# Fourteen tiles of the last feed-forward: rounding the hidden rows one slot later, behind a maximum

## What is computed

```
x = x + cross_attention(layernorm(x), ctx)      # 16 heads of 16, keys and values from the 1601 context rows
x = x + gated_recurrence_and_ff(layernorm(x))   # conv, linear recurrence, gated feed-forward
x = x + bitlinear(gelu(bitlinear(layernorm(x), w1)), w2)

def bitlinear(x, w):                            # the inner rows are 1024 wide
    scale = 127 / max(|x|, per row)
    return (round(x * scale) clipped / scale) @ ternary(w).T
```

## Time and profile before

| | |
|---|---|
| median of 3 runs | 2118.18 us (2115.8 to 2119.51) |
| the profiled execution | 2124.54 us, its span 2122.7 us |
| granted TensorE clock, mean | 0.986 of full speed |
| PE busy | 1970.8 us (93%) |
| DVE busy | 1287.4 us (61%) |
| ACT busy | 1050.8 us (50%) |
| POOL busy | 672.6 us (32%) |

### The profile page before, as it was taken

One profiled execution on the slowest core, in us unless ns is written; L12 is line 12 of the kernel. 1 busy time (PEld: TensorE's weight loads), 2 busy tenths in 40 slices (PEclk: granted clock), 3 DMA queues, 4 the chain that ended last, 5 costly groups with the idle time before them and its releaser, 6 DMA issues.

```text
span 2122.7 us, 72750 instructions
## 1 busy us (share of the span) xinstructions
PE 1970.8 (93%) x31780; PEld 1587.3 (75%) x31796; DVE 1287.4 (61%) x2276; ACT 1050.8 (50%) x1532; POOL 672.6 (32%) x1349
## 2 busy tenths in 40 slices
PE   6799999999999999999999999999999998999987
PEld 4577777777778787787878778787777777777764
DVE  3555656756656665766656575665656666565644
ACT  3444455555465555455555544555544444444441
POOL 4323333423233332333324233342323232122301
PEclk8999999999999999999999999999999999999999
DMA  5533434343333343434333425242342321213122
GB/s 185 183 126 119 146 118 137 104 136 126 123 118 116 120 134 107 133 114 151 121 116 129 134 86 169 74 164 90 113 143 86 119 70 62 78 50 107 50 72 70
DMA packets 124472, 243.92 MB, mean 115 GB/s; under 512 B 13952, under 2 KB 44800, under 8 KB 124160
## 3 DMA queue, kind: packets, MB, share of 16 engines
q1 hardware_dynamic: 123568, 239.23, 34.4%
q10 hardware_dynamic: 592, 0.04, 0.0%
HBM read 235.94 MB, written 3.15 MB: 113 GB/s over the span
## 4 chain that ended last, share of the span: by engine, by line
PE 75%; DVE 9%; ACT 7%; issue 5%; POOL 2%; DMA 0%; SPq 0%; POOLq 0%; DVEq 0%; ACTq 0%
PE M L816 12%; PE M L823 11%; PE SC L1034 10%; PE SC L1057 8%; PE O L1078 7%; PE X L873 5%; ACT probT L1280 4%; DVE mx L1623 3%; PE SC L1050 3%; PE M L873 3%; PE X L1144 2%; PE M L917 1%; PE X L852 1%; PE M L878 1%; PE X L1118 1%
## 5 line engine op out<-in xcount | busy, mean ns | idle before, releaser
L1623 DVE TENSOR_REDUCE mx<-SC 128x4 f32<-128x1600 f32 (+1 forms) x256 | 466.9, 1824 | 159.5 <-PE SC L1034 156.0
L1280 ACT ACTIVATE probT<-SC 128x2048 f32<-128x2048 f32 (+1 forms) x256 | 398.8, 1558 | 160.6 <-PE SC L1057 160.1
L656 POOL TENSOR_TENSOR rowsT<-raw,rowsT 128x256 fp32r<-128x256 f32 (+1 forms) x512 | 324.1, 664 | 380.4 <-ACT rowsT L1334 380.3
L823 PE MATMUL M<-wvs,rowsT 128*128 128x256 f32 x2496 | 359.3, 293 | 3.3 <-issue 1.8
L816 PE MATMUL M<-rowsT,wks 128*128 128x400 f32 (+1 forms) x1536 | 341.5, 363 | 9.5 <-issue 3.6
L1219 ACT ACTIVATE kT<-M,bk 128x400 f32<-128x400 f32 (+1 forms) x256 | 151.7, 594 | 379.7 <-PE M L816 379.3
L816 PEld LDWEIGHTS M<-rowsT,wks 128*128 128x128 f32 x1536 | 271.3, 191 | 83.5 <-issue 67.4
L823 PEld LDWEIGHTS M<-wvs,rowsT 128*128 128x128 f32 x2496 | 315.7, 192 | 23.6 <-issue 3.5
L1425 DVE TENSOR_TENSOR V<-M,bv 128x512 f32<-128x512 f32 (+1 forms) x224 | 145.4, 649 | 283.5 <-PE M L823 275.3
L1034 PE MATMUL SC<-kT,bdq 32*128 32x400 f32 (+1 forms) x2048 | 246.6, 550 | 27.6 <-ACT probT L1280 23.2
L1078 PEld LDWEIGHTS O<-probT,V 128*17 128x17 f32 x13312 | 193.7, 99 | 81.6 <-issue 77.0
(11 more groups left out here) (275 smaller groups left out, 2441.3 us busy)
## 6 DMA issues: line engine op xcount, KB each, us to landing
ring<-in_ws_dram SPq DMA_DIRECT2D x428, 256.0 KB, 4.4
summed<-in_ctx_dram SPq DMA_DIRECT2D x60, 800.5 KB, 4.6
raw<-in_ctx_dram SPq DMA_DIRECT2D x64, 384.0 KB, 4.4
raw<-in_ctx_dram SPq DMA_DIRECT2D x32, 512.0 KB, 4.3
ring<-rounded_scratch SPq DMA_DIRECT2D x64, 256.0 KB, 3.8
raw<-in_ctx_dram SPq DMA_DIRECT2D x32, 321.0 KB, 4.4
out_dram<-x SPq DMA_DIRECT2D x16, 128.0 KB, 2.5
kT<-in_ctx_dram SPq DMA_DIRECT2D x2, 800.5 KB, 8.9
```

Of the source, the lines that this page charges most:

```text
L656: ins = pool.tensor_tensor(rowsT[1][:, c, part], raw[:, c, part], rowsT[0][:, c, part], ALU.subtract)
L823: mm = pe.matmul(bank[:, (t - 2 * a) * D:(t - 2 * a + 1) * D], rowsT[xp][:, cc, t * P:(t + 1) * P], wvs[wp][:, cc, :], start=(at == cc == ...
L1280: act.activation(probT[step % 3][0:w, :, 0:len(ts), :].rearrange("p j t q -> p j (t q)"), SC[0:w, :, 0:len(ts) * P], ACT.Exp)\
L1623: dve.tensor_reduce(mx[c][:, :, n], SC[:, :, 0:KCH[n][1]], AX.X, ALU.max).then_inc(max_used, 1)
```

## The change

For the tiles t = 0 to 13, DVE rounds in `layer1_later` of slot 17, which stands behind slot 17's maximum, and not in slot 16. The 8 transposes "hq" move from slot 17, place D, to slot 18, place B, and the 8 products "down" from slot 18, place B, to slot 18, place D. ACT's copy and DVE's last sum move with them. The row maximum and the scale stay in slot 16. Tiles 14 and 15 keep the places they had. No instruction is added or removed, and no buffer. (The words "scaling and rounding" of the change are lines 1757 and 1758: the product with the scale, then the rounding.)

```diff
 L1_X = {...
-        (15, "B"): "up0", (17, "D"): "hq", (18, "B"): "down"}
+        (15, "B"): "up0", (18, "B"): "hq", (18, "D"): "down"}
+L1_X_LAST = {**{at: kind for at, kind in L1_X.items() if at[0] < 16}, (17, "D"): "hq", (18, "B"): "down"}
...
     for t, q in second_layer(b, k):
-        if (q, place) in L1_X and (L1_X[q, place], t) not in IN_PAIR:
-            yield L1_X[q, place], t
+        at = L1_X if t < NT - 2 else L1_X_LAST
+        if (q, place) in at and (at[q, place], t) not in IN_PAIR:
+            yield at[q, place], t
...
+                    if q == 16 and t != NT - 2:
+                        hidden_max(t)
                     if q == 16:
-                        if t != NT - 2:
-                            hidden_max(t)
                         hidden_scale()
+                    if q == (17 if t < NT - 2 else 16):
                         parts = 2 if t == NT - 1 else 1
```

## The result

The changed kernel takes 2145.25 us (median of 6 runs, 2134.8 to 2156.0) against 2118.85 us for the kernel before (6 runs): a ratio of 1.012, 95% interval 1.0098 to 1.0142. The direction was as forecast. The size was not: +26 us instead of +13, above the range. A second set gave 2139.98 us, ratio 1.0088 (1.0061 to 1.0116).

A forecast was written before the change was run, and what follows sets the result against it. The prediction took a slot's ring without slack, its chain 75% on PE, as the bound. Its terms, -10.5 - 1.3 + 13.3 + 11.3 = +12.8 us, added to 2118.2 gave 2131 us, slower by 0.6%, range 2119 to 2139.

The forecast's parts named there:

- (a): End of slot 17: rounding leaves slot 16 and transposes leave slot 17, so the next scores start sooner; 10.5 us gained.
- (b): Start of slot 18: transposes replace the longer last products, which matters only in tiles 1, 5 and 11; 1.3 us gained.
- (c): End of slot 18: the moved last products are covered by nothing, about 0.97 us per tile; 13.3 us lost.
- (d): Start of slot 19: PE waits at line 1106 for bank X, whose drain queues on DVE; 11.3 us lost.
- (e): Queues elsewhere: POOL, the stores and loads have slack and PE's instruction pauses keep their sum; taken as 0.
- PE's wait for mx falls by 4 to 6: Expected sign: PE's wait for the maximum ahead of the next scores falls by 4 to 6 from 17.6 us.
- 10 to 12: Expected sign: a new PE wait at line 1106 for DVE's last sum, in all fourteen tiles, 10 to 12 us total.
- partly covered: Start of slot 19, tiles 7, 8, 9: bank wait partly covered or behind other DVE pieces; 0.42, 0.75, 0.95 us.
- most of the bank's wait is not there: Rival: PE's pauses or pieces outlast DVE's queue everywhere, so only +3 to +5 us, about 2123; chance 0.13.
- the end of slot 18 is room: Rival: DVE, not PE, ends slot 18, so the products fit beside the maximum; -11.8, 2106 us; chance 0.07.
- the change does not do what it says: Rival: slot 17's maximum is late for value drains, not the rounding; +19 us, 2138 or a little more; chance 0.10.

The follow-up runs named there:

- r9: Kernel before, with the hidden row's maximum and scale at the end of slot 15 instead of slot 16 in tiles 0 to 13; 2111.08 us, ratio 0.9954.
- r5: Kernel before, with one instruction for the rounding's two in tiles 0 to 13, so values are scaled and clipped but not rounded; 2113.21 us, ratio 0.998.
- r12: The same kernel as r9, run once more against other runs of the kernel before; 2113.55 us, ratio 0.9971.
- r2: The changed kernel run again with no edit; 2139.98 us, ratio 1.0088 against the kernel before.
- r4: Changed kernel, with the attention sums' reciprocal and product one slot earlier, behind slot 17's rounding, in even batches 4 to 30; 2138.86 us, ratio 1.0089.
- r8: The changed kernel with no edit, for a third profile; its four distances took 216.7 us, no run time given.
- r11: The change in 12 of its 14 tiles, with tiles 2 and 7 in the order of the kernel before; 2137.02 us, ratio 1.0062.
- r6: The change for tiles 7 to 13 alone, with tiles 0 to 6 as in the kernel before; 2130.11 us, ratio 1.0045.
- r3: Kernel before, with only the last products and last sum moved to the end of slot 18 in tiles 0 to 13; 2157.98 us, ratio 1.0177.

## Why the prediction was right in its signs and short in size

Forecast and measured, the latter as the mean of three profiles of after less that of three of before:

| term | forecast | measured |
|---|---|---|
| (a) end of slot 17 | -10.5 | -10.3 |
| (b) start of slot 18 | -1.3 | -2.5 |
| (c) end of slot 18 | +13.3 | +14.8 |
| (d) start of slot 19 | +11.3 | +15.7 |
| sum of the four | +12.8 | +17.7 |
| (e) elsewhere | 0 | +10.7 |

*(a)* was right in total, and nearly so in its parts: 8.3 were forecast where DVE was late and 2.2 for the transposes alone (tiles 0, 4, 8 and 12); r9 gains 8.2 with the transposes in place, and the change 2.1 more, 0.44 to 0.56 in each of those four. Within this two tiles cancel: tile 4 was late for the rounding as well (0.57 in r5) and gained 1.0 for 0.54, and tile 11 gained 1.5 for 2.2. What it was said to look like was wrong: "PE's wait for mx falls by 4 to 6". Where transposes left, PE waits in their place (0.35 became 0.65 in tile 13); in r5 and r9, which keep them, the wait does fall, to 14.2. A wait in the list is not the price of a half slot.

*(b)* was right at the higher clock. The further 1.2 us are tile 11's, and they are a stretch at the lower clock that all three profiles of before have in its slots 17 and 18 and none of after. r9 and r12, which leave the transposes where they were and have no such stretch, take 4.95 us for the start of slot 18; the changed kernel takes 4.53, that is 0.42 less, for the 0.43 forecast.

*(c)* 0.88 per tile in the bare tiles 12 and 13, not 0.97, since the value products now hand over 0.09 sooner (2007.70 to 2009.62 against 1988.81 to 1990.82). The products themselves still take 0.97 from their start to that of the scores (2009.62 to 2010.59), not the 0.87 that is an estimate by the Trainium skill, "TensorE: Matmul & The Clock Gate", section "Back-to-back issue gap". The sum is larger for another reason. In the first profile tiles 2, 4 and 8 pay 2.2 to 2.6 each, while 0, 6 and 7 pay nothing. In tiles 0, 4, 6 and 7 this goes with pauses of PE for which the profile shows no releaser ("issue"), which appear (1.28 us in tile 4) or go (1.26 becomes 0.35 in tile 0). In tile 2 the value products pause for 1.0; in r2, where they don't, PE waits 0.87 us for ACT's copy at line 1326, which stands behind the delayed softmax, as the rows of r4 show at greater length. In tile 8 it is the lower clock over the value products, 1.6 us, in two of the three profiles; without it (c) is 13.7 for the 13.3 forecast.

*(d) is one of the two terms that failed*, by 4.4 us; the other is (e), by 10.7. The mechanism of (d) was right (r4), and so was the bare price: 1.28 per tile in tiles 12 and 13 for the 1.25 given, and 10.8, 12.6 and 11.7 us of wait for "10 to 12". The 0.42 for tile 7 was not: its start of slot 19 grew by 2.9 us in the profiled execution, 5.2 in r2 and 5.1 in r8. Of this PE's wait is 2.78, 2.23 and 2.24. The rest in r2 and r8, 2.8 us, is the lower clock behind the wait: lines 825 and 875 take 2.90 and 3.5 us there for 1.66 and 1.95. That is 1.9 of the 4.4 in the mean of three, and tile 2 in r2 is another 0.4; at the higher clock (d) is 13.4. The other tiles nearly cancel and were not all right: tile 4 was given 1.25 and paid 0.3 like its neighbours, tile 2 paid 1.9 for 2.6, tile 8 0.4 for 0.75, and tiles 0, 9 and 11 paid 1.0, 1.5 and 1.7 for 0.27, 0.95 and 1.25. For tile 7, "partly covered" was read off the places of DVE's pieces as they ran before. Tile 7 after:

```profile
1252.11 1.03 PE L862 MATMUL X<-ring,arena 128*128 128x256 bf16 x8
1252.32 0.84 ACT L1336 ACTIVATE rowsT<-raw 128x768 fp32r<-128x768 f32 x1
...
1253.24 2.40 POOL L658 TENSOR_TENSOR rowsT<-raw,rowsT 128x128 fp32r<-128x128 f32 x4 [4.23 <-ACT rowsT L1336]
1253.30 0.67 DVE L1640 TENSOR_TENSOR oT<-osb,oT 128x256 f32<-128x256 f32 x1
1253.89 0.74 DVE L1542 TENSOR_TENSOR ggt<-ggt,geq 128x64 f32<-128x64 f32 x1
1254.66 0.22 DVE L1543 TENSOR_REDUCE grank<-ggt 128x16 f32<-128x64 f32 x1
1254.92 0.75 DVE L1544 TENSOR_SCALAR grank<-grank 128x16 f32<-128x16 f32 x1
1255.71 0.17 DVE L1545 TENSOR_SCALAR goff<-grank 128x16 f32<-128x16 f32 x1
1255.79 0.48 DVE L1452 SCALAR_TENSOR_TENSOR x<-X,es,x 128x256 f32<-128x256 f32 x1
1256.33 0.23 PE L1108 MATMUL X<-identb,mparts 128*128 128x128 bf16 x1 [2.78 <-DVE x L1452]
```

and before:

```profile
1237.36 0.42 DVE L1638 TENSOR_TENSOR oT<-osb,oT 128x256 f32<-128x256 f32 x1
...
1237.70 0.22 DVE L1540 TENSOR_TENSOR ggt<-ggt,geq 128x64 f32<-128x64 f32 x1
...
1238.21 0.17 DVE L1542 TENSOR_SCALAR grank<-grank 128x16 f32<-128x16 f32 x1
```

Four routing pieces stand between the reciprocal's product and the last sum, and POOL's work (lines 656 and 658), which before began behind them at 1238.63, now runs beside them: 0.42, 0.22 and 0.17 us became 0.67, 0.74 and 0.75. That growth is 1.35 of the 2.78 us of wait; the rest is the queue itself, which was taken for covered. That POOL lengthens the pieces is read from these rows; no run moves POOL's work away. A queue on DVE was priced in the lengths its instructions had under another neighbour. r11 confirms the size of the two tiles together.

*(e) is the larger term that failed*, and the one that put the time outside the range: it was taken as 0, for reasons that speak of queues of transfers and of PE's pauses, and the clock stands in no term of the sum. That no queue of transfers would matter held: PE waits for no transfer in either kernel. PE's "issue" pauses kept their sum too: 35.0, 29.0 and 31.0 us in the profiles of before, 36.9, 31.5 and 32.6 in those of after. But 10.7 us are outside the moved slots. 6.8 lie in "until", where the order of both kernels is the same and the clock is not: 51 us at the lower level in each of three profiles of after, 17 to 41 in those of before. The windows of after,

```profile
0.00:130.00 130.00, 96.90 (x839) 74.05 (x843) 51.94 (x78) 49.12 (x80) 44.53 (x95) 0.80 0.50 169
```

and of before (the value ahead of the last two is the granted clock):

```profile
0.00:130.00 130.00, 93.72 (x1003) 71.49 (x1004) 58.74 (x87) 53.01 (x84) 46.25 (x101) 0.93 0.49 170
```

r5 has 344.1 there as well without any of the change, and r9 and r12, one kernel, have 341.2 at 31 us of low clock and 343.2 at 48. So part of it is drawn with an execution. Whether some of it belongs to the built kernel, as three equal profiles suggest, stays open. A line fitted to the times and mean clocks of all executions, with a level of its own for each kernel, gives 1.55 us per 0.001 of mean clock. The three profiles of after have a mean clock of 0.979 and those of before 0.985; by the line, an estimate, this is some 10 of the 28.4 us between them. Over all executions the difference is smaller: 0.9816 in 13 of the changed kernel, 0.9833 in 95 of the kernel before, which is worth 2.6 us. By the same line, at one clock, the changed kernel is 18 to 22 us slower than before (r11 15, r6 11), and r9 and r12 are 4 to 6 us faster. The four distances without their stretches at the lower clock give 15.5 (-10.3 - 1.3 + 13.7 + 13.4), so that some 3 to 6 us of the loss have no cause shown. A line through runs is no experiment, and no run here sets the clock.

Of the rivals, "most of the bank's wait is not there" and "the end of slot 18 is room" fell by the first profile, "the change does not do what it says" by r5. The range ended too low because the rest of the program was taken at 0 and single tiles at their covered price. With the measured four distances in place of the +12.8 the forecast would have been 2136 us, inside the range, and the measured time still outside. The bounds given for (d), up to 17.5, would have held its 15.7.

That the sum of the four came within 5 us, and within 3 at the higher clock, is in part luck: apart from tile 7, errors of up to 1 us in single tiles have both signs in (a) and (d).

## What to carry to other kernels

Work that is late in a ring of engines is worth moving to where its engine waits, and only that work: here the inner rows' maximum and scale one slot earlier gain 0.3 to 0.5%, while the rounding one slot later gains 10 us at the end of slot 17 and loses 30 through the products and the drain that have to follow it. Before a drain is put behind other work, list what stands ahead of it on its engine, tile by tile, and who else will be running then, as prices taken under the old neighbours don't hold. And a wait that disappears from the list need not be a gain, nor one that stays a sign of none: take the distances between two starts of the ring. Look at the granted clock over each distance before you explain it by the order: three of the differences here that looked like the order's, in tiles 7, 8 and 11, were wholly or in part the clock's. A range for a change of 0.6% has to hold what the clock can add.

## What was not expected of the hardware

- **DVE beside POOL.** Small DVE instructions grew by 0.25 to 0.58 us each while a POOL group of four (2.40 us in all, line 658) ran: 0.42 to 0.67, 0.22 to 0.74 and 0.17 to 0.75 above. A reduction beside it kept its 0.22. The rounding's two, 0.93 and 0.83 us in slot 16 beside four such POOL instructions that took 3.16 us in all (2.25 in tile 7 before), take 0.74 and 0.69 in slot 17 of tile 13; there two small POOL instructions beside them take 0.65 each, for 0.20 elsewhere. The Trainium skill, "SBUF — State Buffer", section "SBUF: two separate sides", says that GpSimd's instructions share a pair of ports with DVE instructions in a two-port mode, and with those with two SBUF inputs where GpSimd reads SBUF, and that the first to start holds the pair for its whole instruction. The rows agree: the growth is no more than the length of one POOL instruction of the group, and the one-input reduction is spared.
- **The lower clock behind a wait.** In r2, PE stood 2.23 us ahead of line 1108 in tile 7, and the granted clock fell to the lower level. It is the value ahead of the last two: 1.00 in the 7 us up to 1254.00 and 0.58 in the 7 us behind, 0.50 from 1255.10 on.

```profile
1254.00:1261.00 7.00, 5.24 (x25) 5.25 (x26) 2.90 (x8) 0.76 (x2) 1.86 (x4) 0.58 0.39 123
...
1255.76 0.29 PE L1108 MATMUL X<-identb,mparts 128*128 128x128 bf16 x1 [2.23 <-DVE x L1452]
1255.86 2.90 PE L825 MATMUL M<-wvs,rowsT 128*128 128x256 f32 x12
```

The twelve products took 2.90 us for the 1.66 of the same twelve in the profiled execution of after (1256.42), at the higher level. r2, r8 and r3 have this stretch, r3 behind a wait of 2.78 us, and the profiled execution of after, with a wait of the same 2.78 us at the same place, has not: the lower clock can follow a wait of this length and need not. Nor does it need one: in tile 8 of that execution the clock fell at 1381.0, with PE busy for 2.69 of the 3 us before.
